# Silu in the routed experts, the second attention's row scaling behind a split, and the ff stage's rows normalized in halves and measured later

## The reference

```python
# layer 0: x = x + s * g
xn = layernorm(x)
s = attention(xn)      # sigmoid(qn kn^T / 16 - log 2048) v, Wo, + bo, then * layerscale
g = silu(moe(xn))      # top 4 of 16 experts per row, and 2 shared experts
#   one expert: (silu(x @ gate.T) * (x @ up.T)) @ down.T
# layer 1: x = x + s * g
xn = layernorm(x)
s = gelu(xn k^T / |xn k^T| * sqrt(2048)) v    # 2048 bank rows
g = silu(ff(xn))       # ternary W1 (1024 x 256), gelu, ternary W2, + b2
```

## Time and profile before

| | us |
|---|---|
| median of 3 runs | 1235.58 (1235.54 to 1235.79) |
| the profiled execution's own time | 1233.56 |
| its span, first to last instruction | 1231.8 |
| PE busy (matmul) | 1195.6 (97%) |
| DVE busy | 875.9 (71%) |
| ACT busy | 553.7 (45%) |
| POOL busy | 423.0 (34%) |

### The profile page before, as it was taken

The page is one execution under the profiler, slowest core; times in us unless marked ns, Lnnn a source line. Parts: engine busy times, 40 slices in busy tenths (PEclk is TensorE's granted clock), DMA queues, the critical chain, the costliest instruction groups (busy, mean ns, idle before and its releaser), DMA issues.

```text
span 1231.8 us, 26611 instructions
## 1 busy us (share of the span) xinstructions
PE 1195.6 (97%) x8888; PEld 851.7 (69%) x8889; DVE 875.9 (71%) x1893; ACT 553.7 (45%) x1050; POOL 423.0 (34%) x376
## 2 busy tenths in 40 slices
PE   5899999999999999999999999999999999999998
PEld 4556566676688888866666667767766666666665
DVE  8697965556668766678889889998765545555554
ACT  6545632333366666665343345666542222222221
POOL 3353777776036460056777742212000000000000
PEclk8999999999999999999999999999999999999999
DMA  9488355553297665522566647541211011101100
GB/s 300 169 336 319 117 172 167 166 187 134 72 290 229 202 193 188 165 82 76 151 208 196 192 137 241 162 138 37 68 52 52 18 35 52 52 0 51 52 18 18
DMA packets 137830, 169.14 MB, mean 137 GB/s; under 512 B 12899, under 2 KB 126710, under 8 KB 135446
## 3 DMA queue, kind: packets, MB, share of 16 engines
q1 hardware_dynamic: 114438, 125.49, 31.2%
q0 software_dynamic: 12368, 33.70, 8.6%
q10 hardware_dynamic: 10944, 8.92, 2.3%
HBM read 84.18 MB, written 83.89 MB: 136 GB/s over the span
## 4 chain that ended last, share of the span: by engine, by line
PE 75%; DVE 14%; issue 6%; ACT 3%; DVEq 1%; DMA 1%; SPq 0%; ACTq 0%
PE bank L1219 25%; PE sums L1275 15%; PE sums L1234 11%; PE bank L1138 7%; PE sums L1148 4%; PE bank L1080 3%; PE bank L1118 3%; DVE reg_w L2162 2%; DVE stat L1880 2%; PE sums L1090 1%; PE sums L1071 1%; DVE reg_e L2152 1%; DVE reg_qk L1835 1%; DVE reg_w L1835 1%; PE bank L1183 1%
## 5 line engine op out<-in xcount | busy, mean ns | idle before, releaser
L2162 DVE TENSOR_SCALAR reg_w<-reg_w 128x512 f16<-128x512 f32 x320 | 148.4, 464 | 200.3 <-ACT reg_w L1659 199.7
L1835 DVE SCALAR_TENSOR_TENSOR reg_w<-reg_w 128x512 f16<-128x512 f32 x320 | 222.7, 696 | 11.0
L1234 PE MATMUL sums<-reg_v,reg_w 128*128 128x256 f16 x1536 | 188.1, 273 | 1.6 <-DVE reg_w L1835 1.6
L1275 PE MATMUL sums<-reg_v,reg_w 128*128 128x256 f16 x1536 | 188.3, 273 | 0.0
L1219 PE MATMUL bank<-reg_qk,kbT 128*128 128x512 f16 (+1 forms) x768 | 186.7, 379 | 0.0
L1219 PE MATMUL bank<-reg_qk 128*128 (+1 forms) x768 | 186.6, 379 | 0.0
L1659 ACT ACTIVATE reg_w<-bank 128x512 f32<-128x512 f32 x128 | 76.4, 597 | 241.8 <-PE bank L1219 241.8
L1234 PEld LDWEIGHTS sums<-reg_v,reg_w 128*128 128x128 f16 x1536 | 150.0, 98 | 46.3 <-DVE reg_w L1835 3.1
L1275 PEld LDWEIGHTS sums<-reg_v,reg_w 128*128 128x128 f16 x1536 | 150.2, 98 | 44.3
L1659 ACT ACTIVATE reg_w<-bank,nlogs 128x512 f32<-128x512 f32 x128 | 88.0, 688 | 164.7 <-PE bank L1219 158.3
L863 POOL DMA_INDIRECT reg_e<-yg_d,slot_i x128 | 130.9, 1023 | 46.6 <-issue 34.1
(11 more groups left out here) (241 smaller groups left out, 1661.3 us busy)
## 6 DMA issues: line engine op xcount, KB each, us to landing
xg_d<-kbT SPq DMA_DIRECT2D x18, 1024.0 KB, 4.9
xin<-xg_d SPq DMA_DIRECT2D x72, 256.0 KB, 2.8
yg_d<-xr SPq DMA_DIRECT2D x72, 256.0 KB, 2.2
reg_qk<-in_L_attn_x_dram SPq DMA_DIRECT2D x8, 512.0 KB, 7.7
sh_d<-xin SPq DMA_DIRECT2D x16, 256.0 KB, 2.4
xr<-xn_d SPq DMA_DIRECT2D x32, 128.0 KB, 2.6
reg_e<-sh_d SPq DMA_DIRECT2D x32, 128.0 KB, 2.9
moe_d<-reg_e SPq DMA_DIRECT2D x32, 128.0 KB, 1.9
```

The lines of the kernel that those rows point to most:

```text
L1234: mm = pe.matmul(sums[:, bass.ds((c & 1) * (2 * 512) + q * D, D)], (ah, al)[x][:, j % 4, q * P:(q + 1) * P], m.second(y, j), start=(j == 0 ...
L1275: mm = pe.matmul(a_bank[2 * i + q // 2][:, (q % 2) * D:(q % 2 + 1) * D], part[:, j % 4, q * P:(q + 1) * P], m.second(y, j), start=(j == 0 ...
L1835: ins = dve.scalar_tensor_tensor(out=out_ap, in0=in_ap, scalar=scale, in1=hi_ap, op0=ALU.mult, op1=ALU.subtract)
L2162: dve.tensor_scalar(ah[:, j % 4, :], att[:, j % 2, :], m.split, None, ALU.mult).then_inc(m.hi_done, 1)
```

## The change

Three independent parts.

1. In the routed experts ACT computes Silu in place of the sigmoid. DVE's product with the gate half (L2064) and its semaphore chain `t1` go. Two activations of one column are added on ACT, one of Silu before the stage and one of Sigmoid behind it.
2. In the second attention the scaling of chunk c - 1 is issued behind DVE's split of step 2 of chunk c, for c = 1, 2, 3; the last chunk is scaled in the evacuation as before. In the first attention nothing moves, except that a wait stands inside `scale_rows`.
3. In the ff stage `norm_x1` is issued in halves: row groups 0 and 1 at step 7, groups 2 and 3 at step 0 of the next chunk. On DVE `add_up` moves from steps 0 and 1 to steps 1 and 2, and all four `row_stats` to step 3.

```diff
         eb_b = sb("eb_b", [P, E])
         nlogs = sb("nlogs", [P, 1])
         mhalf = sb("mhalf", [P, G4])
+        no_rows = sb("no_rows", [P, 1])
...
             def sigmoid_gate(expert, c, i):
                 m, (sg, t1, hh, hT), h_bank = expert
                 act.wait_ge(m["gu"], at(c))
-                act.wait_ge(m["t1"], at(c - 2))
+                act.wait_ge(m["h"], at(c - 2))
                 act.activation(sg[:, i, :].rearrange("p (e c) -> p e c", e=2),
                                s_bank[i][:, :].rearrange("p (e c) -> p e c", e=2)[:, :, 0:IM],
-                               ACT.Sigmoid, scale=1.0 / QK_PS).then_inc(m["sig"], 1)
+                               ACT.Silu, scale=1.0 / QK_PS).then_inc(m["sig"], 1)
...
+                act.activation(no_rows[:, 0:1], onesf[:, 0:1], ACT.Silu)
                 for c in range(2):
                     rows_hi(c, c % 2)
...
                 rows_out(NSLOT_T // 2 - 1, 3, NSLOT_T // 8 - 1)
+
+                act.activation(no_rows[:, 0:1], onesf[:, 0:1], ACT.Sigmoid)
...
-            def norm_x1(c):
+            def norm_x1(c, halves=(0, 1)):
                 i = c % 2
-                act.wait_ge(q4["nmr"], at(c))
-                act.wait_ge(q4["nn"], at(2 * (c - 3) + 1))
-                act.wait_ge(q4["qs"], at(c - 3))
-                for m in range(G4):
+                if 0 in halves:
+                    act.wait_ge(q4["nmr"], at(c))
+                    act.wait_ge(q4["nn"], at(2 * (c - 3) + 1))
+                    act.wait_ge(q4["qs"], at(c - 3))
+                for m in (m for h in halves for m in (2 * h, 2 * h + 1)):
...
-                ins.then_inc(q4["xn"], 1)
+                if 1 in halves:
+                    ins.then_inc(q4["xn"], 1)
...
             def side(c, j):
-                if j == 0 and c > 1:
-                    queries_hi(c - 2, 1, s_bank[3])
+                if j == 0:
+                    if c > 1:
+                        queries_hi(c - 2, 1, s_bank[3])
+                    if c and c + 1 < NCH:
+                        norm_x1(c + 1, (1,))
...
                 elif j == 7 and c + 2 < NCH:
-                    norm_x1(c + 2)
+                    norm_x1(c + 2, (0,))
...
                 dve.wait_ge(m["sig"], at(c))
-                dve.tensor_tensor(t3, sg[:, i, :].rearrange("p (e c) -> p e c", e=2), ps[:, :, 0:IM], ALU.mult
-                                  ).then_inc(m["t1"], 1)
-                dve.wait_ge(m["t1"], at(c))
                 dve.wait_ge(m["tr"], at(c - 2))
-                dve.scalar_tensor_tensor(out=hh[:, i, :].rearrange("p (e c) -> p e c", e=2), in0=t3,
-                                         scalar=H_S / (QK_PS * QK_PS), in1=ps[:, :, IM:2 * IM],
+                dve.scalar_tensor_tensor(out=hh[:, i, :].rearrange("p (e c) -> p e c", e=2),
+                                         in0=sg[:, i, :].rearrange("p (e c) -> p e c", e=2),
+                                         scalar=H_S / QK_PS, in1=ps[:, :, IM:2 * IM],
                                          op0=ALU.mult, op1=ALU.mult).then_inc(m["h"], 1)
...
                         split(c, j)
+                        if j == 2 and m is at_mix[1] and not first_step(c):
+                            scale_rows(m, c - 1, 1 - i)
                         if at_step:
                             at_step(c, j)
...
                 ins.then_inc(m.evac_read, 1)
+
+
+                if (m is at_mix[0]) != (isinstance(c, int) and c == m.nch - 1):
+                    scale_rows(m, c, i)
+
+            def scale_rows(m, c, i):
+                rows_ = at_rows[at_mix.index(m)][i]
                 dve.wait_ge(m.evac_read, at(m.ch(c)))
...
                 if c + 2 < NCH:
-                    if j < 2:
-                        add_up(c + 2, range(2 * j, 2 * j + 2))
-                    if j in (1, 3):
-                        row_stats(c + 2, range(j - 1, j + 1))
+                    if j in (1, 2):
+                        add_up(c + 2, range(2 * j - 2, 2 * j))
+                    elif j == 3:
+                        row_stats(c + 2)
                     elif j == 4:
                         row_moments2(c + 2)
```

More of the change, by code:

```diff
@@ L438, in build @@
         pj = {n: sem(f"pj_{n}") for n in ("mm", "mv", "ve", "rs", "nmr", "qkn", "vhi", "vlo", "tr", "qhi", "qlo")}
-        steps = ("xt", "xh", "xl", "gu", "sig", "t1", "h", "tr", "hi", "lo", "dn", "ev")
+        steps = ("xt", "xh", "xl", "gu", "sig", "h", "tr", "hi", "lo", "dn", "ev")
         shx = {n: sem("shx_" + n) for n in ("gu", "sig", "h", "hi", "lo", "dn", "ev")}
@@ L1828, in _ @@
                   *(pj[n] for n in ("mv", "ve", "nmr", "vlo", "qlo")),
-                  shx["h"], *(rex[n] for n in ("t1", "h", "lo")), rex["xl"], cb_step, cb_done,
+                  shx["h"], *(rex[n] for n in ("h", "lo")), rex["xl"], cb_step, cb_done,
                   *(q4[n] for n in ("x1", "mv", "ve", "nmr", "l1", "nn", "l2")), bk_b2, bk_silu,
@@ L2061, in inner @@
                 ps = s_bank[i][:, :].rearrange("p (e c) -> p e c", e=2)
-                t3 = t1[:, i, :].rearrange("p (e c) -> p e c", e=2)
                 dve.wait_ge(m["sig"], at(c))
-                dve.tensor_tensor(t3, sg[:, i, :].rearrange("p (e c) -> p e c", e=2), ps[:, :, 0:IM], ALU.mult
-                                  ).then_inc(m["t1"], 1)
-                dve.wait_ge(m["t1"], at(c))
                 dve.wait_ge(m["tr"], at(c - 2))
-                dve.scalar_tensor_tensor(out=hh[:, i, :].rearrange("p (e c) -> p e c", e=2), in0=t3,
-                                         scalar=H_S / (QK_PS * QK_PS), in1=ps[:, :, IM:2 * IM],
+                dve.scalar_tensor_tensor(out=hh[:, i, :].rearrange("p (e c) -> p e c", e=2),
+                                         in0=sg[:, i, :].rearrange("p (e c) -> p e c", e=2),
+                                         scalar=H_S / QK_PS, in1=ps[:, :, IM:2 * IM],
                                          op0=ALU.mult, op1=ALU.mult).then_inc(m["h"], 1)
@@ L2129, in routed_experts @@
                 slot_rows_lo(2, 0)
-                scale_rows(at_mix[0], 1)
+                scale_rows(at_mix[0], S // CW - 1, 1)
                 by(dve, NSLOT_T // 2, 4, one_step, head=32)
@@ L2242, in evac_attention @@
                 ins.then_inc(m.evac_read, 1)
+                if (m is at_mix[0]) != (isinstance(c, int) and c == m.nch - 1):
+                    scale_rows(m, c, i)
+            def scale_rows(m, c, i):
+                rows_ = at_rows[at_mix.index(m)][i]
                 dve.wait_ge(m.evac_read, at(m.ch(c)))
-                if m is at_mix[0] and isinstance(c, int) and c == m.nch - 1:
-                    return
-                scale_rows(m, i)
-            def scale_rows(m, i):
-                rows_ = at_rows[at_mix.index(m)][i]
                 for h in range(2):
```

## The result

The median is 1224.9 us over 4 runs (1224.42 to 1227.15), against 1235.68 for the kernel before beside it (4 runs, 1235.54 to 1236.1): a ratio of 0.9916, 95% interval 0.9899 to 0.9933. Timed again with 5 runs against 20 of the kernel before it was 1225.64 against 1234.94 (0.9928, 0.9914 to 0.9941). The profiled execution took 1224.77, with a span of 1223.0 us; the span is 8.8 shorter than before.

A forecast was written before the change was run, and what follows sets the result against it. PE was taken as the bound, 97 to 98% busy in the three changed stages, so only its waits for DVE counted. Gains of 1.15 + 1.9 + 3.2 = 6.2 us took the median from 1235.58 to 1229.4, range 1226.9 to 1233.6.

The forecast's parts named there:

- The terms for head and end: Routed experts: the earlier product shortens PE's wait by 0.7 us at the stage's head and 0.45 at its end.
- In 70 steps nobody waits for them: worth nothing: Routed experts: the DVE products removed between head and end gain 0 us, since PE never waits for them there.
- Table loads: ACT, around the routed experts: both added loads fit in idle time, cost 0, bounds 0 and 1.4 us.
- the row of 1.40: Earlier trace of ACT: next work starts 1.40 us after a table load starts, small activation included; taken as the load's price.
- rival B: ACT's table switches cost 2.66 us each, the Trainium skill's figure; total time 1230.3 us; chance 5%.
- Rival D: Routed experts: a table load in each of ACT's 16 loop passes, up to 22.4 us, so slower; chance 6%, other slow causes included.
- the 0.2 given back at step 4 of the last chunk: Second attention: PE comes 1.2 us earlier against a slack of 0.97, so some 0.2 us returns as a wait.
- Rival C: Second attention and ff: parts 2 and 3 only move their waits; 1234 us; chance 9%.
- the return behind GpSimd's product in chunks 3 and 4: ff: new DVE waits for ACT make a cycle of about 18.0 us that holds PE, returning 2 x 0.3 us.
- the replay: ff, step by step with the old distances: two new DVE waits for ACT, 0.33 us at step 1, 0.21 at step 2.
- Rival A: ff is caught in DVE's cycle: chunks 2 to 5 run at 18.3 us, ff gives about 1.1; 1231.4 us; chance 18%.
- The median of 1235.58 lies 2.0 over the profiled execution, and I carry that over: Whole kernel: 2.0 us added to the forecast execution of 1227.4 to give the forecast median of 1229.4.

The follow-up runs named there:

- part 1 alone: Silu, one DVE product less and two added one-column activations, on the kernel before: 1232.17 us (10 runs), ratio 0.9977.
- the pairs without the loop: PE's 70 routed steps all written out, on the kernel before (ratios 0.9977 and 0.9964) and on the changed kernel (0.9938, 0.9918 and 0.9945).
- part 2 alone: Only the scaling moved behind the split of step 2 in the second attention, on the kernel before: 1232.65 us (11 runs), ratio 0.9981.

## Why the prediction was wrong in size and right in direction

- **Part 1, 1.15 forecast, 3.2 measured.** The terms for head and end (0.7 and 0.45) held: 0.7 and 0.46. The step that failed is "In 70 steps nobody waits for them: worth nothing". The waits view was read for DVE's row alone; the row above it, "PE bank L1118 <- issue: 2.8, 4, 0.9", was four pauses at PE's pass changes, and they got shorter, from 1.06, 0.78, 0.77 and 0.86 to 0.87, 0.27, 0.27 and 0.31. That it is Silu's doing the run with part 1 alone shows. How: a wait for DVE stands in PE's instruction stream in every step, also where it ends before PE runs dry, and a product that comes 0.34 later brings 0.7 us back at the last four places (0.9 if scaled to 0.45), with the same work of DVE behind it nothing. That, and the pairs without the loop, account for half of the 1.9 us gained there. The other half stays open. At the first pass change the pause differs by more between executions than it changed (0.19).
- **Table loads, 0 forecast, 0 measured.** Next work comes 1.42 us after the start of the load, as the row of 1.40 said and not 2.66 (rival B falls). Of the two loads, placed where the function is first used, one would cost 1.0 us, so the small activations earn their place at one of the two. Rival D, a load in each pass, didn't happen: the trace has six loads in all.
- **Part 2, 1.9 forecast, 1.90 measured**, with the 0.2 given back at step 4 of the last chunk (0.25; with part 2 alone it was 0, so that term isn't firm). Rival C, waits that only move, falls.
- **Part 3, 3.2 forecast, 3.66 measured.** Chunk 0 gave 0.3 (forecast 0.2), chunk 1 0.46 (0.45), chunks 2 to 5 2.9 net (2.6). The term that was mis-sized is the return behind GpSimd's product in chunks 3 and 4: 0.11 and 0.24, not twice 0.3, because DVE's waits for ACT came out smaller than in the replay. Rival A falls. What did it is the norm in halves; the prediction had counted on both moves.
- **The base.** By the trace the change is 8.8 where 6.2 was summed, so 2.6 of the 4.5 us between 1229.4 and 1224.9 lie in the sum. The other 1.9 are the step "The median of 1235.58 lies 2.0 over the profiled execution, and I carry that over". The profiled execution of before (1233.56) was one at the fast edge of its scatter (20 later runs: 1233.51 to 1236.35); the changed kernel's four runs (1224.42 to 1227.15) happened to lie mostly at its own: that is luck of the draw and no gain. The medians of the larger sets differ by 9.3, not by 10.8.
- **The range** ended at 1226.9 because every unknown was bounded within the waits that the prediction had listed (2.3 for part 1). A stage's whole idle time, DVE's or not, would have been the better bound: by the earlier trace rows, 186.0 - 181.6 = 4.4 us in the routed experts.

## What to carry to other kernels

An engine's "issue" pauses at the ends of its loop passes are not fixed costs: here they got shorter when a product in the loop body came earlier, so a relieved wait can pay although nobody is seen waiting for it. Read such pauses in several executions before one is explained: the change at the first of the four here can't be told from chance. Where two edits are meant to mend one wait, look for the idle time upstream (here DVE's 0.97 for a late gelu): the edit that fills it does the work, the other only moves the wait. Take the difference between a profiled execution and a median as scatter until several traces of one kernel show that it isn't.

## What the runs showed of the hardware

- At a taken branch on PE's instruction stream PE lost 0.3 to 1.1 us with a body of 12 steps, without an instruction packet there in the trace, and 5.3 with one of 24, with packets in the pause. After the 5.3 us of idle time the granted clock of the next 4 us was 0.50, the lower level; the row shows it, with x18 matmuls, and the 4 us behind it have x33. It cost 2.2 us:

```profile
401.00:405.00 4.00, 3.79 (x18) 3.05 (x19) 1.28 (x2) 1.08 (x2) 0.00 (x0) 0.50 0.15 52
```

- In the last three sets of runs PE, DVE and ACT stood still again and again while GpSimd issued its 128 indirect scatters (124 to 299 us). For PE and DVE the profile names no wait ("issue"); that they lacked instructions is a guess. The changed kernel in that state, waits over the whole span, and the window of the scatters:

```profile
PE sums L1235 <- issue: 82.2, 58, 3.8
```

```profile
150.00:330.00 180.00, 58.10 (x250) 26.57 (x251) 24.36 (x46) 14.74 (x25) 118.28 (x120) 0.57 0.33 113
```

PE did 250 matmuls in 180 us in which it does 1275 otherwise, with pauses of up to 3.8 us by issue, and the clock fell to 0.57. It struck the kernel before and every variant alike. The scatters themselves took as long as in the other sets (0.96 us each). One of the chips had run the same kernel without it in an earlier set, so it isn't the chip alone; what sets it off stays open.
- A DVE product of two SBUF tiles, 0.42 us alone, took 1.2 to 4.6 beside GpSimd's work on 128 x 2048; a reduction of one SBUF tile stayed at 0.41 (0.42 at most) beside the same work.
